# The RK4 stage of a four-layer network: linear parts by identity matmul in every evaluation, intermediate values in PSUM

## The chip, the cores and the metric

One core of one Trainium2 chip runs the whole network. The metric is the device time of one execution in microseconds (us), lower being better. Engines are called as the profile does: PE is the tensor engine, PEld its weight load, DVE the vector engine, ACT the scalar engine, POOL the GpSimd engine, SP the engine that issues the DMAs.

## What is computed

A (64, 32, 256) input passes four residual layers: attention with an MLP, a GRU over 32 time steps, a block-attention normalisation, and last the layer that is changed here, 32 time steps of a coupled oscillator, integrated with RK4. Its core, cut from the reference:

```python
def _derivative(q, p, drive, coupling, bias):
    i_couple = jnp.tanh(q) @ coupling.T
    dq = q - q ** 3 / 3.0 - p + drive + i_couple + bias
    dp = EPSILON * (q + ALPHA - BETA * p)
    return (dq, dp)

def _rk4_step(q, p, drive, coupling, bias):
    dq1, dp1 = _derivative(q, p, drive, coupling, bias)
    dq2, dp2 = _derivative(q + 0.5 * DT * dq1, p + 0.5 * DT * dp1, ...)
    dq3, dp3 = _derivative(q + 0.5 * DT * dq2, p + 0.5 * DT * dp2, ...)
    dq4, dp4 = _derivative(q + DT * dq3, p + DT * dp3, ...)
    q_next = q + DT / 6.0 * (dq1 + 2 * dq2 + 2 * dq3 + dq4)
    ...                      # p_next alike, and both clipped to -20 .. 20
```

Step t needs q and p of step t - 1, so the 32 steps are serial, and so are the four evaluations in a step. The state of a step is small: 64 batch rows by 256 features, held as 128 partitions by two chunks of 64 columns.

## The kernel before

Each engine has a program of its own, written out by hand in order; engines meet only through counting semaphores (`rk_dve`, `rk_act`, `rk_pe`, `rk_pool`). The tuples `RK_DVE`, `RK_ACT` and `RK_POOL` give the order of an engine's instructions in a step, and a waiter counts up to a name in such a tuple. `mine("x")` is a wait of DVE for its own earlier instruction x.

An evaluation k runs so. ACT takes tanh of the two chunks of the argument (`th1a`, `th1b`), then the square of the whole (`sq1`). PE multiplies the tanh values with the scaled coupling matrix: `coupled(k, c, kk, ...)` adds the product for output chunk c and input chunk kk. DVE forms `w`, a product of square and argument, and then the next argument chunk by chunk from the coupling sum in PSUM: `q2a`, `q2b` behind evaluation 1, and so on to `qa`, `qb` (tile qraw), the q of the next step before its clip. An fp32 matmul shows as two PE instructions.

What is linear in the state reaches an argument in two ways. In evaluations 2 and 4 PE adds it: `linear(k, z)` multiplies tile Z2 or Z4 with an identity and starts the accumulation with it. In evaluations 1 and 3 DVE adds it: it forms y1 = E1 - w (line 1298) or y3 = Z3 - w (line 1325), and adds the PSUM sum to that (lines 1303, 1330). E1 is formed on POOL (line 1500) from the clipped p of the step before, U2, the base of Z2, on DVE between `qa` and `qb` (line 1342).

Behind evaluations 2 and 4 PE issues four matmuls on an idle bf16 tile (`keep_warm(WARM_RK)`, line 482). `twice` makes a matmul write its chunk two times side by side, so that it streams 128 columns instead of 64; only the last matmul of an accumulation is 64 wide. POOL adds each step's q into the output (line 1479, `store`), and forms U4, m, b4, E1 and U3. All values of the stage lie in SBUF except the coupling sums.

Of the kernel before, what the change touches and what calls it, by code (L numbers as in the profile page):

```python
# [11 lines left out]
P = 128  # L12
# [17 lines left out]
WARM_GRU, WARM_RK, WARM_START = 10, 4, 60  # L30
# [21 lines left out]
for _name, _n in (("ada_b", 12), ("qkv_b", 48), ("out_b", 2), ("ffn_b1", 8), ("ffn_b2", 2), ("b_ih", 6),  # L52
# [31 lines left out]
def rk_pool_count(step, name):  # L84

    return {"E1": 1, "U3": 2}[name] if step < 0 else 1 + at(step, RK_POOL, name)


def build(nc, xT, cond, ada_w, qkv_w, out_w, ffn_w1, ffn_w2, w_ih, w_hh, wk, wo, coup, vecs, out):
# [20 lines left out]
    with ctx:  # L110
# [50 lines left out]
        RKN = ("q", "qraw", "q2", "q3", "q4", "qsq", "w", "w4", "y1", "y3", "Z2", "Z3", "Z4", "t3", "E1", "U2", "U3", "U4",  # L161
               "V3", "V4", "V5", "m", "b4", "s1", "s2", "s3", "s4", "P", "D0", "D1", "D2", "th0", "th1")
# [1381 lines left out]
```

## Time and profile before

| | |
|---|---|
| median of 3 runs | 1054.64 us (1052.38 to 1061.86) |
| the profiled execution | 1055.37 us, span 1053.6 us |
| mean granted TensorE clock | 0.969 of full speed |
| PE / DVE / ACT / POOL busy | 940.0 / 644.2 / 434.4 / 278.5 us |
| first and last q of the RK4 loop | 828.9 and 1049.4 us from the span's start |

The span is what lies between the first and the last instruction of the profiled execution; 1.8 us of its time lie around it. Busy time is a sum over the whole span and tells nothing of a stage; the rows below are of the stage that is changed. A name as `rk_w` stands for a tile of the stage, `rk_q` for q, q2, q3 or q4.

### The profile page before, as it was taken

How to read it: one execution, taken by the hardware profiler on the slowest of the kernel's cores; microseconds unless marked ns; L12 is line 12 of the kernel's file. 1: busy time of each engine (PE TensorE's matmuls, PEld its weight loads, DVE VectorE, ACT ScalarE, POOL GpSimd, SP SyncE). 2: the span in 40 equal slices, each digit the busy share in tenths (PEclk: the TensorE clock that was granted, in tenths of full speed). 3: DMA queues.
4: the chain of work that ended last, by engine and by line, in shares of the span. 5: the costliest groups of instructions: out<-in, count | busy, mean ns of one | idle time of the engine just before them, and what ended most of it. 6: DMA issues, size and time to landing. Idle time of an engine off the chain costs nothing.

```text
span 1053.6 us, 18886 instructions
## 1 busy us (share of the span) xinstructions
PE 940.0 (89%) x7276; PEld 762.6 (72%) x7276; DVE 644.2 (61%) x1701; ACT 434.4 (41%) x1147; POOL 278.5 (26%) x372
## 2 busy tenths in 40 slices
PE   4699999999999999998889888999995488888887
PEld 2577887788787887777556667988853477777776
DVE  4355545454555545454654544667668888888887
ACT  2133322332223322323644444555433555555554
POOL 1645400020002000002044333332211644444443
PEclk9799999999999999999999998999997799999999
DMA  5222000000000000002400000000000000000000
GB/s 203 81 81 81 21 1 1 2 1 1 2 1 2 1 1 1 2 1 81 170 0 0 0 1 1 1 2 1 2 1 1 0 2 21 2 21 2 21 1 21
DMA packets 5030, 21.99 MB, mean 21 GB/s; under 512 B 592, under 2 KB 720, under 8 KB 4432
## 3 DMA queue, kind: packets, MB, share of 16 engines
q1 hardware_dynamic: 4944, 20.82, 5.6%
q8 instruction: 56, 0.92, 0.4%
q14 instruction: 30, 0.25, 0.1%
HBM read 18.72 MB, written 2.10 MB: 20 GB/s over the span
## 4 chain that ended last, share of the span: by engine, by line
PE 62%; DVE 24%; issue 7%; ACT 3%; POOL 3%; DMA 0%; DVEq 0%; POOLq 0%; SPq 0%; ACTq 0%
PE ps L303 37%; PE ps L367 6%; PE ps L503 5%; PE ps L493 3%; PE ps L505 3%; PE ps L356 2%; PE ps L310 2%; DVE rk_Z L1308 1%; DVE frs L1244 1%; DVE rk_w L1295 1%; DVE rk_y L1298 1%; DVE BD L961 1%; DVE rk_q L1330 1%; DVE rk_q L1303 1%; ACT rk_qsq L876 1%
## 5 line engine op out<-in xcount | busy, mean ns | idle before, releaser
L586 PE MATMUL ps<-rk_th,cpc 128*128 128x128 f32 x512 | 106.2, 310 | 43.7 <-ACT rk_th L873 39.7
L303 PE MATMUL ps<-x_hi,W_hi 128*128 128x512 f32 x256 | 109.4, 427 | 18.5 <-DVE x_lo L914 16.3
L586 PEld LDWEIGHTS ps<-rk_th,cpc 128*128 128x128 f32 x512 | 73.1, 193 | 66.6 <-ACT rk_th L873 52.9
L931 DVE SCALAR_TENSOR_TENSOR o_lo<-ps,vec,o_hi 128x512 fp32r<-128x512 f32 x64 | 48.0, 751 | 110.4 <-ACT o_hi L671 110.2
L1357 POOL TENSOR_TENSOR xc<-xc,rs 128x1024 f32<-128x1024 f32 x5 | 13.2, 2643 | 361.3 <-DVE rs L910 221.6
L303 PE MATMUL ps<-x_lo,W_hi 128*128 128x512 f32 x256 | 101.3, 396 | 0.0
L655 ACT ACTIVATE qk<-ps,vec 128x512 f32<-128x512 f32 x64 | 44.0, 688 | 138.8 <-PE ps L303 138.8
L303 PE MATMUL ps<-x_hi,W_lo 128*128 128x512 f32 x256 | 101.2, 395 | 0.0
L920 DVE TENSOR_SCALAR qk<-ps,vec 128x512 f32<-128x512 f32 x64 | 47.5, 742 | 77.9 <-PE ps L303 77.9
L671 ACT ACTIVATE o_hi<-ps,vec 128x512 fp32r<-128x512 f32 x64 | 44.0, 688 | 115.8 <-PE ps L367 115.8
L503 PE MATMUL ps<-ht,hh 128*128 128x128 f32 x512 | 78.1, 285 | 2.3 <-DVE ht L1149 2.3
L585 PE MATMUL ps<-rk_th,cpc 128*128 128x64 f32 x512 | 79.1, 257 | 0.0
L585 PEld LDWEIGHTS ps<-rk_th,cpc 128*128 128x128 f32 x512 | 73.5, 194 | 0.0
L873 ACT ACTIVATE rk_th<-rk_q 128x64 f32<-128x64 f32 x192 | 42.2, 251 | 74.8 <-DVE rk_q L1330 32.8
L367 PE MATMUL ps<-BD,V 128*128 128x128 f32 x512 | 70.4, 281 | 2.2 <-DVE BD L961 2.2
L303 PEld LDWEIGHTS ps<-x_hi,W_hi 128*128 128x128 f32 x256 | 48.9, 191 | 31.5 <-DVE x_lo L914 17.1
L503 PEld LDWEIGHTS ps<-ht,hh 128*128 128x128 f32 x512 | 65.7, 191 | 8.2 <-DVE ht L1149 7.1
L367 PEld LDWEIGHTS ps<-BD,V 128*128 128x128 f32 x512 | 64.4, 191 | 6.7 <-DVE BD L961 2.7
L303 PEld LDWEIGHTS ps<-x_hi,W_lo 128*128 128x128 f32 x256 | 49.1, 192 | 10.4 <-issue 1.9
L303 PEld LDWEIGHTS ps<-x_lo,W_hi 128*128 128x128 f32 x256 | 48.8, 190 | 10.8
L303 PE MATMUL ps<-o_hi,wo_hi 128*128 128x512 f32 x128 | 51.7, 404 | 0.9 <-DVE o_lo L931 0.9
L303 PE MATMUL ps<-W_hi,x_hi 128*128 128x512 f32 x128 | 51.8, 404 | 0.0
(227 smaller groups left out, 2237.6 us busy)
## 6 DMA issues: line engine op xcount, KB each, us to landing
stage<-qkv_w SPq DMA_DIRECT2D x7, 768.0 KB, 4.1
stage<-out_w SPq DMA_DIRECT2D x4, 512.0 KB, 3.8
f_raw<-ffn_w SPq DMA_DIRECT2D x2, 1024.0 KB, 6.6
xorig<-xT SPq DMA_DIRECT2D x1, 2048.0 KB, 8.0
out<-xtb SPq DMA_DIRECT2D x4, 512.0 KB, 3.1
ada_sb<-ada_w SPq DMA_DIRECT2D x1, 1536.0 KB, 8.2
x_all<-xT SPq DMA_DIRECT2D x1, 1536.0 KB, 14.1
BD<-qkv_w SPq DMA_DIRECT2D x1, 768.0 KB, 9.4
```

What stands on the lines that cost most here:

```text
L303: r = pe.matmul(out_, lhsT, rhs, start=first and i == 0, stop=last and i == n - 1)
L367: r = pe.matmul(ps[:, OB[h % 2], i * P:i * P + P], V[:, i, h * DH:h * DH + DH], BD[:, i * HU + h, :], start=True, stop=True)
L493: r = pe.matmul(ps[:, PJ[m % 2], :], (ih_hi if term != 1 else ih_lo)[:, c, ms], (y_hi if term != 2 else y_lo)[:, c, js], start=i % 6 == 0, ...
L503: return pe.matmul(ps[:, bank[c], 0:2 * B], hh[:, k, ms], h_.unsqueeze(1).to_broadcast([P, 2, B]), start=k == 0, stop=k == KC - 1)
L505: return pe.matmul(ps[:, bank[c], 0:B], hh[:, k, ms], h_, start=k == 0, stop=k == KC - 1)
L585: return pe.matmul(ps[:, RK_BANK[k % 2][c], 0:B], w, th, start=first, stop=last)
L586: return pe.matmul(ps[:, RK_BANK[k % 2][c], 0:2 * B], w, twice(th), start=first, stop=last)
L655: act.activation(qk[:, 0, h % 2, :], ps[:, PJ[0], :], ACT.Identity, bias=col("qkv_b", HU * u + h)).then_inc(act_evac, 1)
L671: act.activation(o_hi[:, h % 2, :], ps[:, OB[h % 2], :], ACT.Identity, bias=col("qkv_b", 2 * HEADS + HU * u + h)).then_inc(ohi_done, 1)
L873: act.activation(rk[f"th{k % 2}"][:, c, :], rk[src][:, c, :], ACT.Tanh).then_inc(rk_act, 1)
L920: dve.tensor_scalar(qk[:, 1, h % 2, :], ps[:, PJ[1], :], col("qkv_b", HEADS + HU * u + h), None, ALU.add).then_inc(dve_evac, 1)
L931: dve.scalar_tensor_tensor(o_lo[:, h % 2, :], ps[:, OB[h % 2], :], col("qkv_b", 2 * HEADS + HU * u + h), o_hi[:, h % 2, :].bitcast(F32), A ...
```

## The change

RK4 stage only. In evaluations 1 and 3 PE now adds the linear part too, by `linear(1, "E1")` and `linear(3, "Z3")` ahead of the coupling matmuls; y1 and y3 are gone, and the next argument is formed from the PSUM sum and w. The idle matmuls behind evaluations 2 and 4 are gone. E1 moves from POOL to DVE, between w4 and `qa`; U2 moves from between `qa` and `qb` to behind the clip of q, and Z2 now waits for it. The tiles t3, U2, s1 to s4, qsq and V5 move from SBUF to PSUM (banks 0, 1 and 6, which no matmul of the stage writes). The s chain moves earlier on DVE: s1 ahead of Z3, s2 ahead of Z4, s3 ahead of w3, so that s4 alone is left behind `q4b`. On ACT V5 moves ahead of the tanh of evaluation 1, and the two drive instructions (line 852) from behind the square of evaluation 2 to behind that of evaluation 3. The matmuls' order within an evaluation is as before. The diff, without its hunks on start counts:

```diff
--- before.py
+++ after.py
@@ -27,7 +27,7 @@
 NBLK, BLK = 8, T // 8
 DT, EPSILON, ALPHA, BETA, CLAMP = 0.01, 0.08, 0.7, 0.8, 20.0
 LN_EPS = 1e-6
-WARM_GRU, WARM_RK, WARM_START = 10, 4, 60
+WARM_GRU, WARM_START = 10, 60
 
 
 
@@ -64,12 +64,13 @@
            "z_h1", "zc_n1", "h1")
 GRU_ACT = ("r0", "r1", "z0", "zc0", "n0", "z1", "zc1", "n1")
 GI_STEPS = (4, 9, 13, 18, 22, 27, 31, 36)
-RK_ACT = ("th1a", "th1b", "sq1", "V4", "V5", "th2a", "th2b", "sq2", "Da", "Db", "th3a", "th3b", "sq3", "th4a", "th4b", "sq4", "V3")
-RK_DVE = ("q", "Z2", "w1", "y1", "q2a", "q2b",
-          "t3", "Z3", "w2", "q3a", "s1", "q3b",
-          "Z4", "s2", "w3", "y3", "q4a", "q4b",
-          "s3", "s4", "P", "w4", "qa", "U2", "qb")
-RK_POOL = ("store", "U4", "m", "b4", "E1", "U3")
+RK_ACT = ("V5", "th1a", "th1b", "sq1", "V4", "th2a", "th2b", "sq2", "th3a", "th3b", "sq3", "Da", "Db", "th4a", "th4b",
+          "sq4", "V3")
+RK_DVE = ("q", "U2", "Z2", "w1", "q2a", "q2b",
+          "t3", "s1", "Z3", "w2", "q3a", "q3b",
+          "s2", "Z4", "s3", "w3", "q4a", "q4b",
+          "s4", "P", "w4", "E1", "qa", "qb")
+RK_POOL = ("store", "U4", "m", "b4", "U3")
 POOL_DVE = ("score_vec", "wo_sum", "wqr", "keys0", "keys1", "wo_mean", "wo_c", "rms_inv", "score", "score_max", "score_sub",
             "sum", "recip", "att_mul0", "att_sum0", "att0", "att_mul1", "att_sum1", "att1")
...
@@ -158,8 +159,7 @@
             ("s_at", [P, NBLK, B], F32), ("s_mx", [P, 2, B], F32), ("s_wb", [P, NBLK, B], F32),
             ("att", [P, KC, B], F32), ("wo_c", [P, KC, D], F32), ("wo_m", [P, KC], F32))
         assert g_end <= a_w and l_end <= a_w
-        RKN = ("q", "qraw", "q2", "q3", "q4", "qsq", "w", "w4", "y1", "y3", "Z2", "Z3", "Z4", "t3", "E1", "U2", "U3", "U4",
-               "V3", "V4", "V5", "m", "b4", "s1", "s2", "s3", "s4", "P", "D0", "D1", "D2", "th0", "th1")
+        RKN = ("q", "qraw", "q2", "q3", "q4", "w", "w4", "Z2", "Z3", "Z4", "E1", "U3", "U4", "V3", "V4", "m", "b4", "P", "D0", "D1", "D2", "th0", "th1")
         rk = {}
         off = xtb_end
         for n in RKN:
@@ -173,6 +173,11 @@
         OB = (3, 4)
         YB = (5, 6)
         TB = 7
+
+        RK_PSUM = (("t3", 0, 0), ("U2", 0, 1), ("s1", 0, 2), ("s2", 0, 3),
+                   ("s3", 0, 2), ("s4", 0, 3), ("qsq", 1, 0), ("V5", 6, 0))
+        for n, bank, slot in RK_PSUM:
+            rk[n] = ps[:, bank, KC * B * slot:KC * B * (slot + 1)].rearrange("p (c b) -> p c b", b=B)
 
         RK_BANK = ((SB, OB[0]), (OB[1], YB[0]))
...
@@ -594,38 +599,36 @@
 
             keep_warm(WARM_START)
             pe.wait_ge(id_done, 1)
-            pe.wait_ge(rk0, 2)
+            pe.wait_ge(rk0, 1)
+            def chunks_in_turn(t, k):
+                tanh_done(t, k, "a")
+                coupled(k, 0, 0, False, False)
+                tanh_done(t, k, "b")
+                coupled(k, 0, 1, False, True).then_inc(rk_pe, 1)
+                coupled(k, 1, 0, False, False)
+                coupled(k, 1, 1, False, True).then_inc(rk_pe, 1)
+
+            def chunks_together(t, k):
+                tanh_done(t, k, "a")
+                coupled(k, 0, 0, False, False)
+                coupled(k, 1, 0, False, False)
+                tanh_done(t, k, "b")
+                coupled(k, 0, 1, False, True).then_inc(rk_pe, 1)
+                coupled(k, 1, 1, False, True).then_inc(rk_pe, 1)
+
             for t in range(T):
-                tanh_done(t, 1, "a")
-                coupled(1, 0, 0, True, False)
-                coupled(1, 1, 0, True, False)
-                tanh_done(t, 1, "b")
-                coupled(1, 0, 1, False, True).then_inc(rk_pe, 1)
-                coupled(1, 1, 1, False, True).then_inc(rk_pe, 1)
+                pe.wait_ge(rk_dve, RK_START + at(t - 1, RK_DVE, "E1") if t else RK_START)
+                linear(1, "E1")
+                chunks_together(t, 1)
                 pe.wait_ge(rk_dve, RK_START + at(t, RK_DVE, "Z2"))
                 linear(2, "Z2")
-                tanh_done(t, 2, "a")
-                coupled(2, 0, 0, False, False)
-                tanh_done(t, 2, "b")
-                coupled(2, 0, 1, False, True).then_inc(rk_pe, 1)
-                coupled(2, 1, 0, False, False)
-                coupled(2, 1, 1, False, True).then_inc(rk_pe, 1)
-                keep_warm(WARM_RK)
-                tanh_done(t, 3, "a")
-                coupled(3, 0, 0, True, False)
-                coupled(3, 1, 0, True, False)
-                tanh_done(t, 3, "b")
-                coupled(3, 0, 1, False, True).then_inc(rk_pe, 1)
-                coupled(3, 1, 1, False, True).then_inc(rk_pe, 1)
+                chunks_in_turn(t, 2)
+                pe.wait_ge(rk_dve, RK_START + at(t, RK_DVE, "Z3"))
+                linear(3, "Z3")
+                chunks_together(t, 3)
                 pe.wait_ge(rk_dve, RK_START + at(t, RK_DVE, "Z4"))
                 linear(4, "Z4")
-                tanh_done(t, 4, "a")
-                coupled(4, 0, 0, False, False)
-                tanh_done(t, 4, "b")
-                coupled(4, 0, 1, False, True).then_inc(rk_pe, 1)
-                coupled(4, 1, 0, False, False)
-                coupled(4, 1, 1, False, True).then_inc(rk_pe, 1)
-                keep_warm(WARM_RK)
+                chunks_in_turn(t, 4)
 
 
...
@@ -875,16 +878,18 @@
                 def square(src, factor):
                     act.activation(rk["qsq"][:, :, :], rk[src][:, :, :], ACT.Square, scale=factor ** 0.5).then_inc(rk_act, 1)
 
+                if t:
+                    dve_done("P", t - 1)
+                scaled("V5", K5)
                 tanhs(1, "qraw", t - 1, ("qa", "qb"))
                 dve_done("q")
                 square("q", C_ / 3)
                 scaled("V4", K4)
-                scaled("V5", K5)
                 tanhs(2, "q2", t, ("q2a", "q2b"))
                 square("q2", C_ / 3)
-                drive(t + 2)
                 tanhs(3, "q3", t, ("q3a", "q3b"))
                 square("q3", 2 * C_ / 3)
+                drive(t + 2)
                 tanhs(4, "q4", t, ("q4a", "q4b"))
                 square("q4", C_ / 9)
...
@@ -1260,10 +1265,9 @@
             r_ = {n: rk[n][:, :, :] for n in rk}
             STT = dve.scalar_tensor_tensor
             M, Ad, Su = ALU.mult, ALU.add, ALU.subtract
-            dve.wait_ge(rk_dve, RK_START)
+            dve.wait_ge(rk_dve, RK_START - 1)
             dve.wait_ge(rk_act, 4)
-            STT(r_["U2"], r_["P"], -K2, r_["D0"], M, Ad).then_inc(rk0, 1)
-            dve.wait_ge(rk0, 2)
+            dve.tensor_tensor(r_["E1"], r_["D0"], r_["P"], Su).then_inc(rk_dve, 1)
             for t in range(T):
                 def mine(name, step=t):
                     dve.wait_ge(rk_dve, RK_START + at(step, RK_DVE, name))
@@ -1289,57 +1293,52 @@
                     inc(dve.tensor_scalar(r_["q"], r_["qraw"], CLAMP, -CLAMP, ALU.min, ALU.max))
                 else:
                     inc(dve.tensor_copy(r_["q"], r_["qraw"]))
-                mine("q")
+                inc(STT(r_["U2"], r_["P"], -K2, r_[f"D{t % 3}"], M, Ad))
+                mine("U2")
                 inc(STT(r_["Z2"], r_["q"], 1 - A_ * C_, r_["U2"], M, Ad))
                 act_done("sq1")
                 inc(STT(r_["w"], r_["qsq"], -(C_ + 1), r_["q"], Ad, M))
-                pool("E1", t - 1)
+                a1 = coupling(1, 0)
                 mine("w1")
-                inc(dve.tensor_tensor(r_["y1"], r_["E1"], r_["w"], Su))
-                for c in range(KC):
-                    a1 = coupling(1, c)
-                    if c == 0:
-                        mine("y1")
-                    inc(dve.tensor_tensor(half("q2", c), a1, half("y1", c), Ad))
+                inc(dve.tensor_tensor(half("q2", 0), a1, half("w", 0), Su))
+                inc(dve.tensor_tensor(half("q2", 1), coupling(1, 1), half("w", 1), Su))
 
                 pool("U3", t - 1)
-                inc(STT(r_["t3"], r_["U3"], 2.0, r_["q"], M, Ad))
+                inc(STT(r_["t3"], r_["q"], 0.5, r_["U3"], M, Ad))
+                inc(STT(r_["s1"], r_["q"], W1, r_["V5"], M, Ad))
                 mine("t3")
-                inc(STT(r_["Z3"], r_["q2"], -2 * A_ * C_, r_["t3"], M, Ad))
+                inc(STT(r_["Z3"], r_["q2"], -A_ * C_, r_["t3"], M, Ad))
                 act_done("sq2")
                 inc(STT(r_["w"], r_["qsq"], -C_, r_["q2"], Ad, M))
                 a2 = coupling(2, 0)
                 mine("w2")
                 inc(dve.tensor_tensor(half("q3", 0), a2, half("w", 0), Su))
-                act_done("V5")
-                inc(STT(r_["s1"], r_["q"], W1, r_["V5"], M, Ad))
                 inc(dve.tensor_tensor(half("q3", 1), coupling(2, 1), half("w", 1), Su))
 
                 pool("b4")
+                inc(STT(r_["s2"], r_["q2"], W2, r_["s1"], M, Ad))
                 mine("q3b")
                 inc(STT(r_["Z4"], r_["q3"], 2 * (1 - A_ * C_), r_["b4"], M, Ad))
-                inc(STT(r_["s2"], r_["q2"], W2, r_["s1"], M, Ad))
+                mine("s2")
+                inc(STT(r_["s3"], r_["q3"], W3, r_["s2"], M, Ad))
                 act_done("sq3")
                 inc(STT(r_["w"], r_["qsq"], -2 * C_, r_["q3"], Ad, M))
+                a3 = coupling(3, 0)
                 mine("w3")
-                inc(dve.tensor_tensor(r_["y3"], r_["Z3"], r_["w"], Su))
-                for c in range(KC):
-                    a3 = coupling(3, c)
-                    if c == 0:
-                        mine("y3")
-                    inc(STT(half("q4", c), a3, 2.0, half("y3", c), M, Ad))
-
-                inc(STT(r_["s3"], r_["q3"], W3, r_["s2"], M, Ad))
-                mine("s3")
+                inc(STT(half("q4", 0), a3, 2.0, half("w", 0), M, Su))
+                inc(STT(half("q4", 1), coupling(3, 1), 2.0, half("w", 1), M, Su))
+
+                mine("q4b")
                 inc(STT(r_["s4"], r_["q4"], W4, r_["s3"], M, Ad))
                 mine("s4")
                 inc(dve.tensor_scalar(r_["P"], r_["s4"], C_ * (CLAMP - SHIFT), C_ * (-CLAMP - SHIFT), ALU.min, ALU.max))
                 act_done("sq4")
                 inc(STT(r_["w4"], r_["qsq"], -(C_ + 1) / 3, r_["q4"], Ad, M))
+                mine("P")
+                inc(dve.tensor_tensor(r_["E1"], r_[f"D{(t + 1) % 3}"], r_["P"], Su))
                 a4 = coupling(4, 0)
                 mine("w4")
                 inc(STT(half("qraw", 0), a4, 1 / 3, half("w4", 0), M, Su))
-                inc(STT(r_["U2"], r_["P"], -K2, r_[f"D{(t + 1) % 3}"], M, Ad))
                 inc(STT(half("qraw", 1), coupling(4, 1), 1 / 3, half("w4", 1), M, Su))
 
@@ -1468,11 +1467,9 @@
                                channel_multiplier=1).then_inc(id_done, 1)
 
             pool.wait_ge(p_add, 3)
-            pool.wait_ge(rk_dve, RK_START)
             pool.wait_ge(rk_act, RK_ACT_START)
-            TT(r_["E1"], r_["D0"], r_["P"], ALU.subtract).then_inc(rk_pool, 1)
             TT(r_["U3"], r_["D0"], r_["V3"], ALU.subtract).then_inc(rk_pool, 1)
-            pool.wait_ge(rk0, 2)
+            pool.wait_ge(rk0, 1)
 
             def keep(t):
                 pool.wait_ge(rk_dve, RK_START + at(t + 1, RK_DVE, "q"))
@@ -1496,8 +1493,6 @@
                 pool.wait_ge(rk_pool, rk_pool_count(t, "m"))
                 TT(r_["b4"], r_["U4"], r_["m"], ALU.add).then_inc(rk_pool, 1)
                 if t + 1 < T:
-                    dve_("P")
-                    TT(r_["E1"], dnext, r_["P"], ALU.subtract).then_inc(rk_pool, 1)
                     act_("V3")
                     TT(r_["U3"], dnext, r_["V3"], ALU.subtract).then_inc(rk_pool, 1)
             keep(T - 1)
```

## Rows read from the trace of the kernel before

**Rows 1.** Busy time by stretch: first engines and instruction counts, then PEclk, DMA, GB/s.

```profile
830.00:832.00 2.00, 2.00 (x11) 2.00 (x11) 1.38 (x5) 0.72 (x5) 0.82 (x2) 0.50 0.00 0
...
860.00:890.00 30.00, 26.17 (x216) 23.07 (x216) 26.11 (x111) 17.26 (x76) 13.10 (x26) 1.00 0.05 19
```

**Rows 2.** Timeline of DVE over one step (t = 8): start, duration, line, tiles.

```profile
885.13 0.23 DVE L1289 TENSOR_SCALAR rk_q<-rk_qraw 128x128 f32<-128x128 f32 x1
...
885.73 0.42 DVE L1295 SCALAR_TENSOR_TENSOR rk_w<-rk_qsq,rk_q 128x128 f32<-128x128 f32 x1
886.25 0.36 DVE L1298 TENSOR_TENSOR rk_y<-rk_E,rk_w 128x128 f32<-128x128 f32 x1
886.72 0.35 DVE L1303 TENSOR_TENSOR rk_q<-ps,rk_y 128x64 f32<-128x64 f32 x2
...
888.43 0.22 DVE L1316 TENSOR_TENSOR rk_q<-ps,rk_w 128x64 f32<-128x64 f32 x1
...
888.96 0.28 DVE L1321 SCALAR_TENSOR_TENSOR rk_s<-rk_q,rk_s 128x128 f32<-128x128 f32 x1
889.17 0.29 DVE L1323 SCALAR_TENSOR_TENSOR rk_w<-rk_qsq,rk_q 128x128 f32<-128x128 f32 x1
889.50 0.29 DVE L1325 TENSOR_TENSOR rk_y<-rk_Z,rk_w 128x128 f32<-128x128 f32 x1
889.89 0.36 DVE L1330 SCALAR_TENSOR_TENSOR rk_q<-ps,rk_y 128x64 f32<-128x64 f32 x2
...
890.80 0.23 DVE L1336 TENSOR_SCALAR rk_P<-rk_s 128x128 f32<-128x128 f32 x1
890.95 0.28 DVE L1338 SCALAR_TENSOR_TENSOR rk_w<-rk_qsq,rk_q 128x128 f32<-128x128 f32 x1
...
891.48 0.28 DVE L1342 SCALAR_TENSOR_TENSOR rk_U<-rk_P,rk_D 128x128 f32<-128x128 f32 x1
891.68 0.22 DVE L1343 SCALAR_TENSOR_TENSOR rk_qraw<-ps,rk_w 128x64 f32<-128x64 f32 x1
891.93 0.23 DVE L1289 TENSOR_SCALAR rk_q<-rk_qraw 128x128 f32<-128x128 f32 x1
```

**Rows 3.** Chain that ended last, 876 to 892 us, shares by line.

```profile
by line: issue 8.6%; DVE rk_q L1330 6.7%; DVE rk_y L1325 5.7%; DVE rk_s L1334 5.7%; DVE rk_Z L1308 5.6%; DVE rk_w L1295 5.3%; ACT rk_th L873 4.8%; DVE rk_y L1298 4.6%; DVE rk_q L1303 4.4%; DVE rk_P L1336 4.2%; DVE rk_qraw L1341 4.2%; DVE rk
```

**Rows 4.** Timeline of PE over the same step, merged runs of matmuls.

```profile
885.10 0.71 PE L586 MATMUL ps<-rk_th,cpc 128*128 128x128 f32 x4
885.65 0.56 PE L585 MATMUL ps<-rk_th,cpc 128*128 128x64 f32 x4
886.04 0.66 PE L590 MATMUL ps<-rk_Z,ident 128*128 128x128 f32 x4
...
888.05 0.33 PE L585 MATMUL ps<-rk_th,cpc 128*128 128x64 f32 x2
888.23 0.39 PE L482 MATMUL ps<-idle 128*128 128x128 bf16 x4
888.63 0.71 PE L586 MATMUL ps<-rk_th,cpc 128*128 128x128 f32 x4
...
891.23 0.33 PE L585 MATMUL ps<-rk_th,cpc 128*128 128x64 f32 x2
```

**Rows 5.** Instructions on tile q: duration min/median/max ns, first and last start.

```profile
L1295 DVE SCALAR_TENSOR_TENSOR rk_w<-rk_qsq,rk_q x32: 279/416/418, 829.7 to 1043.2; 128x128 f32<-128x128 f32 x32
...
L1313 DVE TENSOR_TENSOR rk_q<-ps,rk_w x32: 224/225/225, 833.0 to 1045.5; 128x64 f32<-128x64 f32 x32
```

**Rows 6.** Timeline, same step: b4 on POOL, the square of evaluation 3 on ACT.

```profile
887.68 0.58 POOL L1497 TENSOR_TENSOR rk_b<-rk_U,rk_m 128x128 f32<-128x128 f32 x1
...
888.85 0.29 ACT L876 ACTIVATE rk_qsq<-rk_q 128x128 f32<-128x128 f32 x1
```

**Rows 7.** DVE groups, 560 to 828 us (GRU): count, busy us, mean ns.

```profile
L1135 DVE TENSOR_TENSOR pn<-rn,gi 128x64 f32<-128x64 f32 x64 | 14.2, 221 | 1.1
...
L1121 DVE TENSOR_TENSOR ar<-ps,gi 128x64 f32<-128x64 f32 x64 | 14.0, 225 | 25.3 <-PE ps L505 16.6 <-ACT gi L782 8.7
```

More of the change, by code:

```diff
@@ L84, in rk_pool_count @@
 def rk_pool_count(step, name):
-    return {"E1": 1, "U3": 2}[name] if step < 0 else 1 + at(step, RK_POOL, name)
+    return 1 + at(step, RK_POOL, name) - (1 if step >= 0 else 0)
 def build(nc, xT, cond, ada_w, qkv_w, out_w, ffn_w1, ffn_w2, w_ih, w_hh, wk, wo, coup, vecs, out):
@@ L244, in start_counts @@
             for s in counts_from_one[name]:
-                engine.sem_inc(s, RK_START - 1 if s is rk_dve else 1)
+                engine.sem_inc(s, RK_START - 2 if s is rk_dve else 1)
         block = ctx.enter_context(nc.Block())
@@ L861, in _ @@
             drive(1)
-            act.wait_ge(rk_dve, RK_START)
+            act.wait_ge(rk_dve, RK_START - 1)
             scaled("V3", K3)
-            act.wait_ge(rk0, 2)
+            act.wait_ge(rk0, 1)
             for t in range(T):
```

## Prediction

> **What bounds the kernel now.** I read the stretches first, then the chain, then the engines' timelines over one step. The changed stage is 32 serial steps, and from 860 us on PE's granted clock is 1.00, its upper level of 2.4 GHz [rows 1]. One step, from one clip of q (885.13) to the next (891.93), takes 6.80 us [rows 2]; 32 of them are a fifth of the span, and outside them only start counts and the first E1 and U2 change. In that stretch PE and DVE are both busy 87% of the time [rows 1], so busy time doesn't say who leads. The chain of waits does: it names DVE lines almost alone, besides the tanh and "issue", and no matmul [rows 3]. The two DVE lines that the change removes are in it, y3 with 5.7% and y1 with 4.6%. But a chain names only one of two nearly equal paths, so I need for each evaluation the DVE path and the PE path apart.
>
> Three habits of the timeline carry the sums. A dependent DVE instruction starts 0.03 us after the end of what it needs (qb ends 891.90, q starts 891.93), and 0.10 after it where it stands behind two waits (w1 ends 886.15, y1 starts 886.25; y3 ends 889.79, q4a starts 889.89). An independent one follows at a pitch shorter than its duration: 0.21 for 128 columns (s2 at 888.96, w3 at 889.17), 0.15 behind the clip-like P (890.80 to 890.95) [rows 2]. DVE starts 0.04 after the last matmul it needs: line 585 ends at 888.38 and q3b starts at 888.43 [rows 2, 4].
>
> I cut the step at the points where something new decides: q of step t, then q2a, q3b, q4a, qb, and the next q.
>
> **Evaluation 1, q to q2a: now 886.72 - 885.13 = 1.59.** Today w1, which waits for the square, starts at 0.60 and takes 0.42, y1 starts at 1.12 and takes 0.36, q2a starts at 1.59 [rows 2]. In its place: U2 is queued behind q at the pitch, 0.14, lasts 0.28 (its row, 891.48) to 0.42; Z2 waits for it, 0.46; w1 follows at the pitch, 0.67, which is 0.07 later than the square would allow. This is the price of the moved U2, and it is on the path. w1 then loses a slowing: its median is 416 ns but its shortest 279 [rows 5], and POOL works on q beside it in all steps but the first. With qsq in PSUM it has one SBUF input, like q3a, which runs shortly ahead of q3b while POOL forms b4 (887.68 to 888.26, rows 6) and lasts 224 to 225 ns in all 32 steps [rows 5]. I take 0.28, bound 0.42. So w1 ends at 0.95, and q2a, which needs it behind two waits, starts at 1.05. Saved: 0.54; with w1 at its upper bound 0.40. The Trainium skill, page "SBUF — State Buffer", section "Who interferes with whom", has a rule for it: a DVE instruction with two SBUF inputs contends with a GpSimd instruction that reads SBUF, one with a single SBUF input doesn't. By that rule w1 is free of it and U2 itself, with P and D both in SBUF, is exposed; its row of today shows 0.28. By the rule the sum below stands; by the row's upper bound for w1 it is 4 us less.
>
> Is PE ready? Both halves of the sum must be there at 1.05 and 1.20. E1, one pitch behind w4, ends by 890.95 + 0.21 + 0.29 = 891.45 even on today's times [rows 2], and w4 comes sooner once s3 is out of its way. Four identity matmuls last 0.66 to the end of the last; coupling's four, behind a wait, last 0.71 and hand over after 0.55 (885.10 to 885.65), so I take 0.50 of queue time for `linear`, and 0.45 for coupling's four where no wait holds them. PE's queue is free 0.15 before its last matmul ends (888.23 against 888.38). So `linear(1)` starts at 891.56 - 0.15 = 891.41 and is done at 891.91, just where coupling starts today (885.10 + 6.80) [rows 4]. Today the second half is ready at 886.21 + 0.04, 1.12 behind q; less the 0.10 of the wait, and with q 0.07 earlier (below), 1.09. Covered by 0.1.
>
> **Evaluation 2, q2a to q3b: 1.71, unchanged.** q3b starts right at the end of PE's last matmul (888.38), whose order and start stay. The faster Z3, the earlier s1 and t3 in PSUM move only q3a. Nothing saved.
>
> **Evaluation 3, q3b to q4a: now 889.89 - 888.43 = 1.46.** y3 goes. s2, Z4, s3 follow q3b at 0.14, 0.35, 0.56, w3 at 0.77; the third square ends at 889.14 [rows 6] and would let it start at 0.74, as now. w3 lasts 0.29, two waits 0.10: q4a at 1.15. Saved: 0.31. PE must now fit `linear(3)` in. It is free at 888.23, where its idle matmuls start [rows 4], 1.51 behind q2a; plus 0.50 is 2.01, later than the 1.91 (888.63) at which the tanh lets coupling start now [rows 4]. From there 0.45 and two matmuls' 0.33 and the 0.04: first half at 2.83 behind q2a; DVE wants it at 1.71 + 1.15 = 2.86. So PE and DVE arrive here within 0.03 of each other; a slip of PE's goes straight into the time. The second half comes 0.23 later (0.56 for four against 0.33 for two, rows 4), at 3.06, and q4b follows 0.19 behind q4a instead of 0.14; evaluation 4 has its waits ahead of its first half, so this is hidden.
>
> **Evaluation 4, q4a to qb.** s3 is gone from the way to P and w4, so `qa` comes sooner, though E1 takes a slot of 0.21 there. The second half decides: PE ends at 891.56 [rows 4] and `qb` could start at 891.61; today U2, issued at 891.48, holds it to 891.68 [rows 2]. Saved: 0.07, and not more, since PE's order is the same. V5 ahead of the tanh takes one more slot on ACT between P and `qa`, while DVE spends there 0.15 to w4, 0.21 each to E1 and `qa`, and 0.22 in `qa` itself: covered. The drive instructions lie in ACT's idle time in either place. POOL, short of E1, holds nobody up.
>
> **The sum.** 0.54 + 0.31 + 0.07 = 0.92 a step: 6.80 becomes 5.88. In the first step PE has its lower clock (0.50, which is 1.2 GHz) and is busy without a pause [rows 1]; there two `linear` in place of eight idle matmuls cost about what DVE saves, by estimate, so I count nothing for it. 31 x 0.92 = 28.5 us off the profiled 1055.37, which is 0.7 above the median: 1026.9, say 1027. What a measurement of this kernel can tell from no change is about 1%, 10.5 us.
>
> **Unknown prices.** No row shows DVE writing PSUM. A read costs next to nothing: 225 ns against 221 for the same shape [rows 7]. By that nearest row I take zero. The upper bound is a second fixed cost on every write: a 64-column instruction lasts 0.22 and a 128-column one 0.28 to 0.29, so the fixed part is about 0.15. On the path lie U2 to Z2 (0.15) and s2 to s3 (0.15 less the 0.10 of slack); the rest is hidden by PE: 0.20 a step, 6 us, 1033. Below nothing, a PSUM write could be quicker; U2 alone is exposed to that, so 0.05 a step, 1.5 us, is the most I give it.
>
> **Rivals.** (1) *PSUM is dearer for DVE than rows 7 say*, on each access and in the pitch too. Six accesses lie on the path (U2, Z2, w1; s2, s3, w3). Halfway between nothing and the fixed part of 0.15, at 0.075, that is 0.45 a step, 14 us: 1041. For it: no row of a 128-column PSUM operand exists; against it: rows 7. The Trainium skill, "Perfetto Trace Analysis", section "Optimizing Scalar/DVE Operations", gives DVE an overhead of about 60 ns on SBUF and 125 on PSUM; with 65 ns on six accesses an estimate from that page is 12 us lost, 1039. The rows of reads here don't agree with it. Chance 20%. (2) *PE becomes the bound.* Per step it has four `linear` at 0.50 and four couplings at 0.84 to 0.90, about 5.5 of 5.88. If `linear(1)` and `linear(3)` hand over as slowly as a restart, 0.05 to 0.10 each, 0.1 to 0.2 a step come back, 3 to 6 us: 1030 to 1033. For it: slack of 0.03 in evaluation 3. Chance 17%. (3) *Slower: the lower clock.* The idle matmuls go, and if the clock falls in the stage, PE alone decides: 11 instructions took 2.00 us there, 0.18 each [rows 1], and 48 a step need 8.7 against 6.80, so 61 us more if it lasts, 1116. It decides against the change once a third of the steps run so (0.92 of 8.7 - 5.88). Against it: the clock is 1.00 today with more idle than the new order leaves. Chance 4%. (4) *The change doesn't shorten the path*, because E1 or Z3 reaches PE late and evaluation 1 or 3 stands still for it: gain under 1%, 1045 to 1050. Z3 starts about 0.7 behind q2a and PE takes it at 1.5, so this needs a wait I don't see. Chance 4%. The forecast, 1023 to 1031, has the remaining 55%.
>
> The range takes in forecast, rival 2 and rival 1 to its price: 1022 to 1041. Chances: faster 0.92, within 1% 0.04, slower 0.04.
>
> **What would show it.** q to q at 5.9; q2a about 1.05 behind q, q4a 1.15 behind q3b, `qb` on the end of the last matmul. w1 near 280 ns right or wrong shows POOL's part; durations of U2, t3 and the s lines the price of a PSUM write, and a pitch over 0.21 that of rival 1. PE idle before line 590 only in evaluations 2 and 4. The forecast fails if evaluation 2's end is not PE's any more, or if q2a waits for the coupling sum.

## Result, and the profile after

The changed kernel took 1023.24 us (median of 4 runs, 1022.8 to 1027.99) against 1054.70 before; the ratio is 0.971 with a 95% interval of 0.966 to 0.976. Forecast were 1027 and a range of 1022 to 1041. The profiled execution was the slowest of the four, 1027.99, span 1026.3.

First the length of the stage, from the line of `qb` and from the first copy of q (columns: duration min/median/max ns, first and last start us), the changed kernel:

```profile
L1342 DVE SCALAR_TENSOR_TENSOR rk_qraw<-ps,rk_w x32: 214/224/225, 839.7 to 1021.7; 128x64 f32<-128x64 f32 x32
L1295 DVE COPY rk_q<-rk_qraw x1: 473/473/473, 832.0 to 832.0; 128x128 f32<-128x128 f32 x1
```

The kernel before:

```profile
L1343 DVE SCALAR_TENSOR_TENSOR rk_qraw<-ps,rk_w x32: 216/217/219, 837.1 to 1049.1; 128x64 f32<-128x64 f32 x32
L1291 DVE COPY rk_q<-rk_qraw x1: 364/364/364, 828.9 to 828.9; 128x128 f32<-128x128 f32 x1
```

From the copy to the last `qb` the loop took 189.7 us, and 220.2 before. So the stage gave 30.5 us, more than the 27.4 by which the two profiled executions differ: in the changed one the stage began 3.1 us later. Its start lies between 823.8 and 836.5 us in the profiled executions of this study, kernels whose earlier stages are the same. The total thus carries several us that have nothing to do with the change, and below I compare the step: the median of the 31 intervals between starts of `qb`. Before 6.80 us, after 5.86; forecast 5.88.

One step on DVE, the changed kernel (timeline; start, duration, line):

```profile
887.05 0.23 DVE L1293 TENSOR_SCALAR rk_q<-rk_qraw 128x128 f32<-128x128 f32 x1
887.19 0.29 DVE L1296 SCALAR_TENSOR_TENSOR ps<-rk_P,rk_D 128x128 f32<-128x128 f32 x1
887.51 0.29 DVE L1298 SCALAR_TENSOR_TENSOR rk_Z<-rk_q,ps 128x128 f32<-128x128 f32 x1
887.72 0.28 DVE L1300 SCALAR_TENSOR_TENSOR rk_w<-ps,rk_q 128x128 f32<-128x128 f32 x1
888.11 0.23 DVE L1303 TENSOR_TENSOR rk_q<-ps,rk_w 128x64 f32<-128x64 f32 x1
...
889.82 0.22 DVE L1316 TENSOR_TENSOR rk_q<-ps,rk_w 128x64 f32<-128x64 f32 x1 [0.22 <-PE ps L590]
...
890.55 0.28 DVE L1325 SCALAR_TENSOR_TENSOR rk_w<-ps,rk_q 128x128 f32<-128x128 f32 x1
890.94 0.22 DVE L1328 SCALAR_TENSOR_TENSOR rk_q<-ps,rk_w 128x64 f32<-128x64 f32 x1
...
891.75 0.29 DVE L1334 TENSOR_SCALAR rk_P<-ps 128x128 f32<-128x128 f32 x1
...
892.65 0.22 DVE L1342 SCALAR_TENSOR_TENSOR rk_qraw<-ps,rk_w 128x64 f32<-128x64 f32 x1
892.90 0.23 DVE L1293 TENSOR_SCALAR rk_q<-rk_qraw 128x128 f32<-128x128 f32 x1
```

Read against [rows 2] at the same points: q to q2a 1.06 (was 1.59), q2a to q3b 1.71 (1.71), q3b to q4a 1.12 (1.46), q4a to `qb` 1.71 (1.79), `qb` to q 0.25 (0.25). They add up to 5.85.

The same step on PE:

```profile
886.62 0.71 PE L595 MATMUL ps<-rk_E,ident 128*128 128x128 f32 x4
887.17 0.61 PE L591 MATMUL ps<-rk_th,cpc 128*128 128x128 f32 x4
887.62 0.56 PE L590 MATMUL ps<-rk_th,cpc 128*128 128x64 f32 x4
888.01 0.66 PE L595 MATMUL ps<-rk_Z,ident 128*128 128x128 f32 x4
888.67 0.49 PE L591 MATMUL ps<-rk_th,cpc 128*128 128x128 f32 x2
...
890.96 0.66 PE L595 MATMUL ps<-rk_Z,ident 128*128 128x128 f32 x4
891.50 0.49 PE L591 MATMUL ps<-rk_th,cpc 128*128 128x128 f32 x2
```

A group of four 128-column matmuls hands over to the next after 0.50 where nothing holds it (its last starts 0.39 in, the next 0.11 later). After 888.01 the next group starts at 888.67 and not at 888.51, after 890.96 at 891.50 and not at 891.46: PE waits 0.16 and 0.04 for a tanh there. The other handovers are at the pitch (the regular distance between two starts), save the start of `linear(1)`, which is held 0.04 for E1. But the busy time and the chain of the changed kernel say something else (windows as in [rows 1]; then the chain from 876 to 892 us):

```profile
860.00:890.00 30.00, 30.00 (x248) 28.61 (x247) 25.92 (x123) 19.77 (x86) 11.63 (x26) 1.00 0.05 19
```

```profile
by line: PE ps L591 39.4%; PE ps L595 35.5%; PE ps L590 25.7%
```

PE is busy 30.00 of 30.00 us, and the chain is PE from end to end. A 128-column matmul's row lasts 0.28 to 0.38 while the next starts after 0.11, so a wait of 0.16 vanishes under the row before. Two readings were left, and to tell them apart was the first question. Theory A, the one of the prediction: the step is a ring, from q through the four evaluations back to q, and DVE's instructions in evaluations 1 and 3 are links of it that count in full, as PE's in 2 and 4. Theory B, as these two views have it: PE's queue alone is the bound.

### The profile page after: what moved, and what is told of

The parts are those of the page before. It is cut to its first block, busy times and chain, and to the rows that moved or that the text cites. A ratio compares the mean times of both kernels' runs of the same rounds, so it can differ in the third digit from the quotient of the medians.

```text
span 1026.3 us, 18758 instructions
## 1 busy us (share of the span) xinstructions
PE 944.8 (92%) x7276; PEld 781.0 (76%) x7276; DVE 617.0 (60%) x1669; ACT 434.0 (42%) x1147; POOL 254.7 (25%) x340
## 4 chain that ended last, share of the span: by engine, by line
PE 78%; issue 8%; DVE 8%; POOL 3%; ACT 2%; DMA 1%; POOLq 0%; SPq 0%; DVEq 0%; ACTq 0%
PE ps L308 36%; PE ps L591 7%; PE ps L595 6%; PE ps L508 6%; PE ps L372 5%; PE ps L590 4%; PE ps L498 3%; PE ps L510 3%; PE ps L315 2%; PE ps L361 2%; DVE frs L1249 1%; PE ps L396 1%; POOL xc L1361 1%; DVE BD L966 1%; DVE g_lo L1075 1%
## 5 line engine op out<-in xcount | busy, mean ns | idle before, releaser
L591 PE MATMUL ps<-rk_th,cpc 128*128 128x128 f32 x512 | 98.9, 296 | 0.1
L876 ACT ACTIVATE rk_th<-rk_q 128x64 f32<-128x64 f32 x192 | 44.8, 254 | 53.6 <-DVE rk_q L1315 22.4
L595 PE MATMUL ps<-rk_Z,ident 128*128 128x128 f32 x384 | 64.2, 290 | 0.0
```

What stands on the lines that cost most here:

```text
L591: return pe.matmul(ps[:, RK_BANK[k % 2][c], 0:2 * B], w, twice(th), start=first, stop=last)
L595: pe.matmul(ps[:, RK_BANK[k % 2][c], 0:2 * B], ident[:, :], twice(rk[z][:, c, :]), start=True, stop=False)
L876: act.activation(rk[f"th{k % 2}"][:, c, :], rk[src][:, c, :], ACT.Tanh).then_inc(rk_act, 1)
```

## The experiments

All are edits of the changed kernel but e13. A step is the median over the one profiled execution of that kernel; ratios are to the kernel before. The totals follow the steps only roughly: e2's median is 15 us above the changed kernel's, its loop 10.6 us longer (200.3 against 189.7). So the readings below rest on steps and rows, not on totals.

| kernel | step us | median us | ratio, 95% interval |
|---|---|---|---|
| before / changed | 6.80 / 5.86 | 1054.7 / 1023.2 | 0.971 (0.966 to 0.976) |
| e1 y1 back | 6.36 | 1039.3 | 0.982 (0.977 to 0.988) |
| e2 y3 back | 6.19 | 1038.5 | 0.981 (0.976 to 0.987) |
| e3 all eight tiles in SBUF | 6.48 | 1043.5 | 0.986 (0.981 to 0.992) |
| e4 U2 between qa and qb | 6.09 | 1032.4 | 0.975 (0.969 to 0.981) |
| e5 idle matmuls back | 6.10 | 1031.9 | 0.977 (0.971 to 0.982) |
| e8 all matmuls 64 columns | 10.24 | 1163.9 | 1.104 (1.097 to 1.110) |
| e9 e4, U3 behind U2 | 6.03 | 1027.9 | 0.973 (0.968 to 0.978) |
| e10 e9, s4 in SBUF | 5.96 | 1030.2 | 0.973 (0.965 to 0.980) |
| e11 e10, U3 behind q | 5.78 | 1023.9 | 0.972 (0.966 to 0.978) |
| e12 64 columns in part | 5.87 | 1023.4 | 0.973 (0.966 to 0.979) |
| e13 before, squares in PSUM | 6.76 | 1054.9 | 1.000 (0.997 to 1.004) |
| e14 squares in SBUF | 5.88 | 1023.1 | 0.970 (0.963 to 0.977) |

**e1 and e2: ring or queue.** Each gives PE an identity group less and DVE one instruction more.

```diff
-                linear(1, "E1")
-                chunks_together(t, 1)
+                chunks_together(t, 1, True)      # starts the accumulation itself
...
+                inc(dve.tensor_tensor(r_["y1"], r_["E1"], r_["w"], Su))
-                inc(dve.tensor_tensor(half("q2", 0), a1, half("w", 0), Su))
+                inc(dve.tensor_tensor(half("q2", 0), a1, half("y1", 0), Ad))
```

e2 does the same to evaluation 3, with y3 = 2 Z3 - w.

> The changed kernel, with evaluation 1 as it was: no linear(1), y1 = E1 - w on DVE. Step of the changed kernel: 5.86 us. Theory A (the ring runs through DVE: q to q2a 1.06, q3b to q4a 1.12, and through PE twice for 1.71): q2a comes 0.33 later (y1's 0.29 and a dependent start), up to 0.40 if POOL slows y1; step 6.19 to 6.26, 10 to 12 us slower than the changed kernel. Theory B (PE's queue is the bound, as the chain of the changed kernel names PE alone): PE loses the 0.5 to 0.6 us of linear(1), so the step stays at 5.86 or gets shorter.

> The changed kernel, with evaluation 3 as it was: no linear(3), y3 = 2 Z3 - w on DVE. Theory A: q4a comes 0.33 later, step 6.19, 10 us slower than the changed kernel. Theory B: PE loses 0.5 us, the step stays at 5.86 or gets shorter.

e2 measured 6.19, 0.33 more than the changed kernel, as theory A says to the hundredth. e1 measured 6.36, 0.50 more where A expected 0.33 to 0.40. Theory B wanted no increase and falls: PE had 0.5 us less to do, and the step grew by what DVE got. The chain went through PE alone although PE waited in each step. The excess in e1 is y1's length (timeline of e1, both engines):

```profile
914.18 0.46 POOL L1490 TENSOR_TENSOR rk_U<-rk_D,rk_V 128x128 f32<-128x128 f32 x1
914.33 0.46 DVE L1300 TENSOR_TENSOR rk_y<-rk_E,rk_w 128x128 f32<-128x128 f32 x1
```

y1 started 0.15 after POOL's U4 and ended at 914.79, 0.15 after U4's end. In e2 no POOL instruction ran beside y3 (timeline of e2):

```profile
915.75 0.29 DVE L1325 SCALAR_TENSOR_TENSOR rk_y<-rk_Z,rk_w 128x128 f32<-128x128 f32 x1
```

**e3: the tiles back in SBUF.** `RK_PSUM` is emptied and the eight names go into `RKN`.

> The changed kernel with all eight tiles (t3, U2, s1 to s4, qsq, V5) in SBUF again. Theory A: w1 reads two SBUF tiles beside POOL again, 0.42 instead of 0.28, and this is on the ring: step 6.00, 4.3 us slower; Z3 slower too, but hidden by PE; P 0.07 quicker, hidden. The rival (PSUM is dear for DVE): the step gets shorter by up to 0.2 us. Theory B: nothing on DVE counts, step 5.86.

Step 6.48: 0.62 more, and 0.14 was expected. A rival with dear PSUM wanted a shorter step and is excluded, but my size was four times too small. w1, on which I had put it all, is quick; three others are slow (DVE groups by form of e3, 850 to 1010 us: busy us, mean ns):

```profile
L1307 DVE SCALAR_TENSOR_TENSOR rk_s<-rk_q,rk_V 128x128 f32<-128x128 f32 x24 | 13.6, 568 | 0.0
L1311 DVE SCALAR_TENSOR_TENSOR rk_w<-rk_qsq,rk_q 128x128 f32<-128x128 f32 x24 | 12.9, 539 | 0.0
L1297 DVE SCALAR_TENSOR_TENSOR rk_Z<-rk_q,rk_U 128x128 f32<-128x128 f32 x25 | 11.2, 448 | 0.9
...
L1299 DVE SCALAR_TENSOR_TENSOR rk_w<-rk_qsq,rk_q 128x128 f32<-128x128 f32 x25 | 7.0, 279 | 0.0
```

**e4: U2 back between `qa` and `qb`**, so that Z2 waits for q alone.

```diff
-                inc(STT(r_["U2"], r_["P"], -K2, r_[f"D{t % 3}"], M, Ad))
-                mine("U2")
+                mine("q")
...
+                inc(STT(r_["U2"], r_["P"], -K2, r_[f"D{(t + 1) % 3}"], M, Ad))
                 inc(STT(half("qraw", 1), coupling(4, 1), 1 / 3, half("w4", 1), M, Su))
```

> The changed kernel with U2 back between qa and qb, so that Z2 needs only q. Theory A: w1 can start at 0.57 behind q instead of 0.67, qb starts about 0.05 later: step 5.81, 1.5 us faster. Theory B: w1 doesn't matter, a later qb does little either: step 5.86. Third possibility: U2 costs qb more than it gives w1, as it would have with w1 held by the square: step 5.9.

Step 6.09, 0.23 more; all three expectations missed. Timeline of e4:

```profile
923.68 0.46 POOL L1499 TENSOR_TENSOR rk_U<-rk_D,rk_V 128x128 f32<-128x128 f32 x1 [2.93 <-ACT rk_V L859]
923.71 0.58 DVE L1343 SCALAR_TENSOR_TENSOR ps<-rk_P,rk_D 128x128 f32<-128x128 f32 x1
```

U2 started 0.03 after POOL's U3, lasted 0.58 and ended 0.15 after U3's end. Before the change it stood in the same place and lasted 0.28 [rows 2]: E1 on POOL held U3 back to 891.52, behind U2's start at 891.48, and E1 itself ended at 891.57, too early to matter. From e1, e3 and e4 I formed the rule that replaces "POOL slows w1", and call it the lock: a DVE instruction with two SBUF inputs that starts while a POOL instruction runs ends 0.15 after that one, if this is later than its own end; one that starts first isn't touched, and a POOL instruction that starts within 0.04 behind it gets longer (0.55 to 0.58 against 0.46 in the kernel before). With one input in PSUM there is no lock: Z2 of the changed kernel, whose U2 lies in PSUM, starts 0.16 behind POOL's store and lasts 0.29; in e3, with U2 in SBUF, 0.45. The Trainium skill, page "SBUF — State Buffer", section "Who interferes with whom", states that a DVE instruction with two SBUF inputs contends with a GpSimd instruction that reads SBUF, and that issue order decides who blocks. The traces agree: 0.45 against 0.29 for Z2, 0.58 against 0.28 for U2.

**e5: the idle matmuls back** (`keep_warm(WARM_RK)` behind evaluations 2 and 4).

> The changed kernel with the four idle matmuls back behind evaluations 2 and 4. They take 0.22 us of PE's queue each time. Theory A (ring through DVE and PE, PE with 0.16 us of slack before the coupling of evaluation 2 and 0.05 before that of evaluation 4, and q4a waiting for PE and DVE at the same time): behind evaluation 2 the idle matmuls push linear(3) and with it q4a by 0.22; behind evaluation 4 they push linear(1) by 0.18 but q2a by 0.03 only: step 6.11, 8 us slower. Theory B (PE's queue alone): 0.44 a step, 6.30. If they cost nothing, their removal was no part of the change.

Step 6.10, 0.24 more: theory A again (6.11). Behind evaluation 2 the idle matmuls start where `linear(3)` could, and it comes 0.22 later (timeline of e5):

```profile
919.33 0.39 PE L487 MATMUL ps<-idle 128*128 128x128 bf16 x4
919.55 0.66 PE L595 MATMUL ps<-rk_Z,ident 128*128 128x128 f32 x4
```

So taking them out was needed to fit `linear(3)` in.

**e8: every matmul of the stage 64 columns wide** (the `twice` of `coupled` and `linear` removed).

> The changed kernel with every matmul of the stage 64 columns wide (none streams its chunk twice). Theory A: in evaluations 2 and 4 coupling ends 0.17 sooner, q3b and qb with it; evaluations 1 and 3 keep their 1.06 and 1.12 on DVE: step 5.52, 11 us faster, if the clock stays at its upper level. Theory B: PE's queue gets 1.4 us shorter, so the step falls until DVE binds, 5.5 as well. Rival: with half the columns the granted clock falls to 1.2 GHz in the stage and the step is 6 us or more.

The rival came true, step 10.24 (windows of e8, as in [rows 1]):

```profile
900.00:930.00 30.00, 30.00 (x143) 30.00 (x142) 15.20 (x71) 11.56 (x49) 6.35 (x14) 0.50 0.05 18
```

PE's granted clock is 0.50, 1.2 GHz, through the whole stage, with PE busy 30.00 of 30.00 us; in the changed kernel it rose to 1.00 in the first step. Matmuls start every 0.21 us in e8.

**e9, e10, e11: getting POOL out of the way.** e9 is e4 with POOL's U3 started behind U2.

> U2 between qa and qb as in e4_u2_between, where it lasted 583 ns beside POOL's U3 and the step was 6.09. Here POOL starts U3 only after U2 is done. Lock theory (U2 with two SBUF inputs stood still until POOL's U3 ended): U2 lasts 0.28 to 0.29, qb comes 0.05 later than in the changed kernel, w1 0.10 sooner: step 5.81 to 5.86. Rival (U2 is slow there for its place between two reads of PSUM): U2 still lasts 0.5 or more, step 6.1.

```profile
915.20 0.29 DVE L1343 SCALAR_TENSOR_TENSOR ps<-rk_P,rk_D 128x128 f32<-128x128 f32 x1
915.40 0.22 DVE L1344 SCALAR_TENSOR_TENSOR rk_qraw<-ps,rk_w 128x64 f32<-128x64 f32 x1
915.57 0.46 POOL L1500 TENSOR_TENSOR rk_U<-rk_D,rk_V 128x128 f32<-128x128 f32 x1 [3.32 <-ACT rk_th L876]
915.65 0.46 DVE L1295 TENSOR_SCALAR rk_q<-rk_qraw 128x128 f32<-128x128 f32 x1
```

In this timeline of e9 U2 is back at 0.29, so the lock theory holds for it and the rival (its place) falls. But the step is 6.03: now q, started 0.08 after U3, lasts 0.46 instead of 0.23. q is a tensor_scalar with one SBUF input; it is caught as well, and ends 0.08 after U3. My expectation had left it out.

> e9_u2_first with s4 in SBUF, all other tiles as in the changed kernel. P, a tensor_scalar, reads s4: it lasted 0.29 from PSUM and 0.23 from SBUF. Theory: P's duration goes back to 0.23 and w4, E1, qa and U2 follow 0.07 sooner, so that qb waits for PE alone: step 5.76, 3 us faster than the changed kernel. If qb was PE's already: as e9_u2_first.

Step 5.96, not 5.76: P went to 0.23 and `qb` to PE's end as expected, but q is caught in this kernel too (duration min/median/max ns):

```profile
L1295 DVE TENSOR_SCALAR rk_q<-rk_qraw x31: 405/408/455, 839.6 to 1018.9; 128x128 f32<-128x128 f32 x31
```

e11 changes POOL's order to U3, U4, m, b4, store, with U3 waiting for q:

```diff
-RK_POOL = ("store", "U4", "m", "b4", "U3")
+RK_POOL = ("U3", "U4", "m", "b4", "store")
...
+                if t:
+                    pool.wait_ge(rk_act, RK_ACT_START + at(t - 1, RK_ACT, "V3"))
+                    dve_("q")
+                    TT(r_["U3"], drow, r_["V3"], ALU.subtract).then_inc(rk_pool, 1)
                 act_("V4")
```

> e10_u2_first_s4 (U2 between qa and qb, s4 in SBUF), with POOL's order changed: U3 only behind the clip q, then U4, m, b4, and the store last. In e10 U3 ran beside q, which lasted 410 ns instead of 226, step 5.96. Lock theory: no instruction of DVE that uses two SBUF ports on the ring has POOL beside it now; q lasts 0.23, w1 starts 0.57 behind q, qb is PE's: step 5.76 to 5.78, 3 us faster than the changed kernel. Rival (PE's queue): coupling of evaluation 2 had only 0.16 of slack, coupling of evaluation 1 behind linear(1) none; if w1's 0.10 runs into that, the step stays near 5.86.

Step 5.78, as expected. Timeline of e11:

```profile
910.01 0.29 DVE L1345 SCALAR_TENSOR_TENSOR ps<-rk_P,rk_D 128x128 f32<-128x128 f32 x1
910.24 0.23 DVE L1346 SCALAR_TENSOR_TENSOR rk_qraw<-ps,rk_w 128x64 f32<-128x64 f32 x1
910.50 0.23 DVE L1295 TENSOR_SCALAR rk_q<-rk_qraw 128x128 f32<-128x128 f32 x1
910.76 0.29 DVE L1299 SCALAR_TENSOR_TENSOR rk_Z<-rk_q,ps 128x128 f32<-128x128 f32 x1
910.87 0.46 POOL L1494 TENSOR_TENSOR rk_U<-rk_D,rk_V 128x128 f32<-128x128 f32 x1 [3.34 <-ACT rk_th L876]
911.07 0.29 DVE L1301 SCALAR_TENSOR_TENSOR rk_w<-ps,rk_q 128x128 f32<-128x128 f32 x1
```

w1 starts 0.57 behind q, nothing on the ring is held, and the stage is 0.09 a step, some 3 us, shorter than in the changed kernel. The total can't tell the two apart (0.972 against 0.971); only the step can.

**e12: 64 columns in the coupling of evaluations 2 and 4 alone.**

> The changed kernel with 64 columns instead of 128 in the coupling matmuls of evaluations 2 and 4 alone; evaluations 1 and 3 and all linear matmuls stream 128 as before. With all of them at 64 the granted clock stayed at 0.50 through the stage and a step took 10.24 us. If the clock rises as in the changed kernel: q3b 0.26 sooner, qb 0.16 sooner (then held by qa), step 5.44, 13 us faster. If it stays at 0.50: PE alone decides, about 10 us a step, over 100 us slower. Theory B gives 5.4 as well.

The clock rose (granted 1.00 from 832 us on), and the step is 5.87: no gain where I expected 0.42. Both theories missed. Timeline of PE in e12:

```profile
907.18 1.11 PE L590 MATMUL ps<-rk_th,cpc 128*128 128x64 f32 x8
```

The eight matmuls take 1.11 to the end of the last; the 128- and 64-column groups of the changed kernel between the same points, 888.67 to 889.78, take 1.11 as well. Within the eight the starts lie 0.11 apart, but for the first, as those of the 128-column ones do, and so do the starts of the weight loads in either kernel. That the loads set this pace is my reading; no run changes them alone.

**e13 and e14: the squares by themselves.** e13 is the kernel before with qsq in PSUM and nothing else, e14 the changed kernel with qsq in SBUF and nothing else.

> The kernel before with one part of the change alone: the squares (qsq) in PSUM. Step before: 6.80. My prediction counted 0.14 for w1, 0.42 to 0.28. If that holds by itself: step 6.66, 4 us faster than before. Lock theory: w1 is quick, 0.28, but y1 (E1 and w, both in SBUF) then starts right when POOL's U4 has the port and ends with it, at the same time as before: step 6.78 to 6.80, no gain.

> The changed kernel with the squares (qsq) alone back in SBUF; t3, U2, the s tiles and V5 stay in PSUM. My prediction took w1 from 0.42 to 0.28 because of this tile: step 6.00 with it back. Lock theory, from the earlier runs: an instruction of DVE with two SBUF inputs ends 0.15 behind the POOL instruction that was running when it started, if that is later than its own end. In the changed kernel w1 starts at 0.67 behind q and POOL's store ends at 0.76, so w1 would end at 0.91 by the lock and at 0.95 by itself; w2 starts at 1.93 and POOL's m ends at 1.95, so it is free too: step 5.86 to 5.90. If w2 slips behind b4 (started at 2.03) it lasts 0.54 as in e3_sbuf, and the step is 6.0 or more for that reason instead.

e13: step 6.76, 0.04 less, and no change in the total. Timeline of e13:

```profile
916.66 0.29 DVE L1298 SCALAR_TENSOR_TENSOR rk_w<-ps,rk_q 128x128 f32<-128x128 f32 x1
916.93 0.46 POOL L1496 TENSOR_TENSOR rk_U<-rk_D,rk_V 128x128 f32<-128x128 f32 x1
917.05 0.48 DVE L1301 TENSOR_TENSOR rk_y<-rk_E,rk_w 128x128 f32<-128x128 f32 x1
```

w1 is down to 0.29, but y1 then runs into U4 and lasts 0.48 instead of 0.36; 6.66 was the price of w1 by itself, 6.78 to 6.80 that of the lock theory, and 6.76 lies by the second. e14: step 5.88, 0.02 more, and w1 (instructions on qsq in e14, min/median/max ns) is quick from SBUF too, as the lock theory had it (5.86 to 5.90, against 6.00 by the prediction's account of w1):

```profile
L1300 DVE SCALAR_TENSOR_TENSOR rk_w<-rk_qsq,rk_q x32: 282/283/286, 824.7 to 1010.2; 128x128 f32<-128x128 f32 x32
```

## Why the prediction was right

**The ring.** The cut at q, q2a, q3b, q4a and `qb` held. The terms: evaluation 1 0.54 forecast, 0.53 measured; evaluation 2 nothing and nothing; evaluation 3 0.31 and 0.34, since w3 follows at pitches of 0.20 and not 0.21; evaluation 4 0.07 and 0.08. The step lost 0.94 for 0.92 forecast. e1, e2 and e5, each off by one piece, gave 0.33 plus a lock, 0.33 and 0.24; the ring forecast these sizes and the queue theory (nothing, nothing, 0.44) did not. That the chain after would show PE alone I hadn't foreseen.

**w1: right number, wrong cause.** I took 0.14 of the 0.54 of evaluation 1 from w1, by the move of the squares to PSUM. e14 has them in SBUF and w1 lasts 0.28 all the same; e13 has the move without the rest and gains 0.04. By the rule of e4 and [rows 2], w1 used to start at 0.60 behind q, inside POOL's store, and ended 0.15 after it. In the changed kernel it starts at 0.67 and the store, begun at 0.30 behind q, ends 0.46 later at 0.76: a lock would let w1 end at 0.91, and by itself it ends at 0.95. What freed w1 is that it comes later, behind U2, and that the store isn't prolonged by Z2 (0.57 before, 0.46 now). The term came out right by luck, through an edit that I had booked as a cost. That U2 costs 0.07 there was right; e4 and e11 show what the place buys: it keeps U2 clear of U3.

**The PSUM tiles.** I had taken them for nothing but w1 and a faster Z3 that is hidden. e3 puts them at 0.62 a step: with the earlier arguments DVE's two-input instructions would fall into POOL's (Z2, s1, w2). The evaluation 1 delay in e3 (q2a 1.22 behind q, against 1.06) is Z2's lock; the rest is w2's, at 0.54, through q3a to PE. So without them two thirds of the step's 0.94 would be lost. What the eight would do to the kernel before by themselves no run shows, but for the squares (e13, 0.04). This part was absent from the forecast, which came out right because no instruction on the ring was held in the changed kernel: luck again, as the prediction set none but w1, q3a and U2 against POOL's work.

**The unknown price.** DVE's write to PSUM costs 0.01 (U2 0.281 before, 0.291 after), a 128-column read 0.004 (w2 279 to 283 ns). Taking zero was right, and rival 1 is out. The Trainium skill's "Perfetto Trace Analysis", section "Optimizing Scalar/DVE Operations", has 65 ns more for PSUM; no instruction with three operands shows that here. One does change by as much: P, a tensor_scalar, lasts 0.29 from PSUM and 0.23 from SBUF (e10). Its extra 0.06 isn't on the path to `qb`, which starts at PE's end.

**Rivals 2 to 4.** PE bound: near, not reached. `linear(3)` fitted, with nothing to spare: q4a starts 0.10 behind w3's end, the gap of two waits, and 0.04 behind PE's last matmul for it, so both were ready within 0.01. The handovers kept the pitch. The lower clock was a real danger: without the idle matmuls it still rose, with all columns at 64 it didn't (e8). Its price had been put too low, at 8.7 a step from 0.18 a matmul; e8 shows 0.21 and 10.24. E1 does reach PE late, 0.04 behind the free queue (P from PSUM delays it: E1 starts 4.75 behind Z2 in e9 and 4.68 in e10); it costs a slower start of 0.09 that the 0.10 of cover takes.

**The first step and the total.** The first step took 7.65 us from the copy of q to `qb` against 8.19 before, where I had counted nothing. That isn't the change's doing, but the clock's. Windows of the first step (columns as in [rows 1]) in the kernel before, in e13, in the changed kernel and in e14:

```profile
828.93:837.12 8.19, 7.79 (x48) 7.60 (x48) 6.07 (x24) 3.99 (x18) 2.76 (x7) 0.65 0.00 0
826.92:834.62 7.70, 7.00 (x48) 6.67 (x48) 6.05 (x25) 3.93 (x18) 2.62 (x7) 0.76 0.00 0
832.01:839.66 7.65, 7.43 (x49) 7.37 (x50) 5.21 (x24) 3.96 (x19) 1.95 (x5) 0.75 0.00 0
823.80:832.41 8.61, 8.38 (x49) 8.32 (x50) 5.26 (x25) 4.03 (x19) 2.01 (x5) 0.66 0.00 0
```

e13 and e14 differ from the first and the third kernel by one tile. At a mean granted clock of 0.75 to 0.76 the old and the new order take 7.70 and 7.65, at 0.65 to 0.66 they take 8.19 and 8.61. Beyond that, the kernel before had five steps 0.1 to 0.3 longer than the median, 1.2 us in all, and the changed one two, 0.4 us. So the 30.5 us of the stage are 29.1 of the step, 0.5 of the clock and 0.8 of such steps. The forecast of 28.5 was right for its step and had neither of the others; the median lies 3.7 us below it, in a part of the range for which the prediction has a term of 1.5 us only.

## What to carry to other kernels

Cut a serial loop into the points where something new decides, and sum each engine's path between them; when two engines are near, remove work from the one that the chain names before believing it, because pipelined matmul rows hid waits of up to 0.16 us here. Between DVE and POOL look at which instruction starts first: an instruction moved by 0.1 us can gain or lose 0.3, so a saving found on one instruction isn't additive, and a tile's move to PSUM is worth what it prevents in the final order. Before counting on a narrower matmul, look at the granted clock and at whether the next one starts sooner at all.

## What the runs showed of the hardware

- A DVE instruction with two SBUF inputs that starts behind a POOL instruction ends 0.15 us after it, where that is later than its own end: y1 0.46, s1 0.57, w2 0.54, U2 0.58 against 0.28 to 0.29 alone. With one of the two in PSUM it isn't held. The plain tensor_scalar q is held as well and ends 0.08 after (0.46 and 0.41 against 0.23).
- With all matmuls 64 columns wide PE was busy without a gap and its clock stayed at 1.2 GHz through the 328 us of the loop; with the coupling of two evaluations at 64 and the rest at 128 it went to 2.4 GHz as before.
- At 2.4 GHz eight matmuls with changing weights take 1.11 us whether four of them stream 128 or all stream 64 columns.
- ACT's square lasts 0.26 us into PSUM and 0.29 into SBUF.
